# Patch attention and three 3x3 convolutions on one core: products without hold products, full products, and turning by scaled diagonals

## What is computed

```python
q = x @ Q_P;  k = stk @ K_P;  v = stk @ V_P      # stk: the 9 shifted views of x
alpha = softmax(sum(k * q) * mask, axis=-1)      # over the 9 neighbours
t = t_in = x + sum(alpha * v)
t = relu(conv(t, ff1) + b1)
t = relu(conv(t, ff2) + b2)
t = relu(conv(t, ff3) + b3)
return t_in + t
```

## Time and profile before

| | |
|---|---|
| median of 3 runs | 2381.85 us (2379.44 to 2382.46) |
| the profiled execution, its own time | 2380.99 us |
| its span | 2379.0 us |
| share of the span: TensorE, VectorE, ScalarE | 96%, 80%, 47% |
| loads of weights on TensorE (beside products) | 55% |
| granted clock of TensorE, mean | 0.993 of full |
| instructions | 65460 |
| 16 DMA engines, mean busy share | 46% |

### The profile page before, as it was taken

How to read it: one execution, slowest core, us unless ns; L and a number is a source line. 1 busy time by engine, 2 the same in 40 slices (tenths; PEclk the granted TensorE clock), 3 DMA queues, 4 the chain that set the end, 5 groups by cost and what they waited for, 6 DMA issues and landing times.

```text
span 2379.0 us, 65460 instructions
## 1 busy us (share of the span) xinstructions
PE 2287.5 (96%) x25180; PEld 1317.7 (55%) x25180; DVE 1895.5 (80%) x2851; ACT 1127.4 (47%) x3108; POOL 15.5 (1%) x24
## 2 busy tenths in 40 slices
PE   4999999999999999999999999999998999999998
PEld 2655555555565555555555555555555555555554
DVE  4888888887588888888768888888877888888886
ACT  1554455444454554454345544544535445444543
POOL 2000000000000000000000000000000000000000
PEclk9999999999899999999999999999999999999999
DMA  4444544544355445444344454445434544454443
GB/s 125 138 137 136 158 134 125 160 141 134 94 158 152 137 126 162 139 136 137 123 138 144 126 160 140 135 136 157 135 124 119 156 147 138 127 160 136 128 153 119
DMA packets 291286, 328.79 MB, mean 138 GB/s; under 512 B 89300, under 2 KB 223252, under 8 KB 284564
## 3 DMA queue, kind: packets, MB, share of 16 engines
q1 hardware_dynamic: 291164, 327.17, 46.4%
HBM read 152.50 MB, written 33.82 MB: 78 GB/s over the span
## 4 chain that ended last, share of the span: by engine, by line
PE 79%; DVE 12%; issue 5%; ACT 1%; DVEq 1%; DMA 1%; SPq 0%; ACTq 0%
PE conv_banks L476 28%; PE conv_banks L435 16%; PE conv_banks L490 15%; PE mix_bank L413 6%; PE score_banks L387 3%; DVE work L836 3%; PE score_banks L398 3%; PE mix_bank L425 3%; DVE dt L764 2%; DVE tf L746 2%; DVE dt L760 2%; PE score_banks L381 1%; PE proj_bank L420 1%; PE score_banks L395 1%; PE conv_banks L450 1%
## 5 line engine op out<-in xcount | busy, mean ns | idle before, releaser
L476 PE MATMUL conv_banks<-dodd,w3f 128*64 128x512 f32 (+1 forms) x1656 | 500.3, 579 | 6.2 <-DVE dodd L760 3.9
L476 PE MATMUL conv_banks<-deven,w3f 128*64 128x512 f32 (+1 forms) x1656 | 489.9, 566 | 0.0
L598 ACT ACTIVATE prob<-score_banks,negmax 128x100 f32<-128x100 f32 x1040 | 343.0, 343 | 273.4 <-DVE negmax L726 273.4
L435 PE MATMUL conv_banks<-dt,w1f 128*64 128x256 f32 (+3 forms) x4224 | 414.4, 384 | 0.0
L490 PE MATMUL conv_banks<-duh,w2h 64*128 64x512 f32 (+2 forms) x1632 | 362.2, 423 | 4.0 <-ACT m_sb L634 2.1
L664 ACT ACTIVATE relued<-work,bias 128x1024 f32<-128x1024 f32 (+2 forms) x136 | 150.4, 1108 | 435.7 <-DVE work L836 435.7
L490 PE MATMUL conv_banks<-duh,w2l 64*128 64x512 f32 (+2 forms) x1632 | 329.5, 382 | 0.0
L435 PEld LDWEIGHTS conv_banks<-dt,w1f 128*64 128x64 f32 (+1 forms) x4224 | 219.2, 135 | 138.6 <-issue 65.9
L490 PE MATMUL conv_banks<-dul,w2h 64*128 64x512 f32 (+2 forms) x1632 | 286.4, 383 | 0.0
L476 PEld LDWEIGHTS conv_banks<-dodd,w3f 128*64 128x64 f32 x1656 | 138.8, 137 | 226.5 <-issue 181.3
L490 PEld LDWEIGHTS conv_banks<-duh,w2h 64*128 64x128 f32 x1632 | 168.7, 185 | 137.7 <-issue 104.5
(11 more groups left out here) (97 smaller groups left out, 3224.2 us busy)
## 6 DMA issues: line engine op xcount, KB each, us to landing
xk<-x_keys SPq DMA_DIRECT2D x66, 800.0 KB
xc<-x_bands SPq DMA_DIRECT2D x66, 650.0 KB, 5.0
dodd<-dodd SPq DMA_DIRECT2D x68, 512.0 KB, 5.1
xr<-x_bands SPq DMA_DIRECT2D x264, 128.0 KB, 3.5
out<-work SPq DMA_DIRECT2D x60, 512.0 KB, 2.7
dt<-dt SPq DMA_DIRECT2D x68, 256.0 KB, 2.3
deven<-deven SPq DMA_DIRECT2D x68, 256.0 KB, 5.7
duh<-duh SPq DMA_DIRECT2D x68, 256.0 KB, 2.4
```

The source lines that it names most:

```text
L435: mm = nc.tensor.matmul(bank[(LOWER, UPPER)[o], n * 256 + lo * 64:n * 256 + hi * 64], w1f[i][rows, m, s, o * C:o * C + C], dt[rows, lo + s ...
L476: return nc.tensor.matmul(bank[rows, lo * 128:hi * 128], w3f[:, m, s, odd * C:odd * C + C], source[:, lo + s // 2:hi + s // 2, m], start=s ...
L598: last = nc.scalar.activation(prob[:, g % 2, a], score_banks[:, g % 2, a * KEYS:(a + 1) * KEYS], ACT.Exp, bias=negmax[:, g % 2, a:a + 1], ...
```

## The change

On TensorE the eight hold products of a step are dropped (single ones stay in the part ahead of the loop). The waits stand by themselves, and those of r, scores, turn and v-product are moved ahead of the last one or more products of what comes before. Of the third convolution tile 1 comes second and 2 third. In the second convolution, where both halves of the rows meet the same product, one full product of 128 by 128 takes the place of two halves: a tile has 6 full products (`begin2`: 4, `end2`: 2) and then 6 half products. `half_done` and its wait go.

`prob` is no longer scaled. VectorE forms one reciprocal for the 8 patches of a half and multiplies an identity with it, which gives 8 diagonal matrices `scaled` of 64 by 64; `turn` multiplies `prob` by them in an ordinary f32 product, where a transpose was. Two loads for the identity come into SP's queue ahead of the biases. On VectorE the outer part of `dt` is formed behind the first outer sum of the next step, and maxima, sums and scaling are put in another order; on ScalarE the copy of r comes first, the copy of the third convolution ahead of the first relu, and the copy of the second convolution's odd tile ahead of the copy of y.

```diff
-    return ORDER3.index(j) if which == CONV3 else 4 + 2 * j + (which == EVEN)
+    return j if which == CONV3 else 4 + 2 * j + (which == EVEN)
...
+            for rows in (LOWER, UPPER):
+                sp.dma_start(eye_two[rows], eye[rows, rows]).then_inc(const_in, 16)
...
+            def hold(bank):
+
+                nc.tensor.matmul(bank[:, 0:2], eye16_sb[:], window_sb[:, 0:2], start=True, stop=True)
+
+            def await_band(b):
+                pe.wait_ge(t_ready, b * 2)
+                pe.wait_ge(xc_in, b * 16 + 16)
+                pe.wait_ge(xs_in, b * 32 + 32)
...
+            def await_r(b, half):
+                pe.wait_ge(r_ready, b * 2 + (half + 1))
+                if half:
+                    pe.wait_ge(probt_ready, b * 2 + 1)
...
             def turn(b, half):
-                pe.wait_ge(prob_ready, b * GROUPS + (2 * half + 2))
-                nc.tensor.matmul(score_banks[:, 0, 0:2], eye_sb[LOWER], eye_sb[LOWER, 0:2], start=True, stop=True)
                 for a in range(HALF):
                     for n, rows in enumerate((LOWER, UPPER)):
-                        last = nc.tensor.transpose(score_banks[0:KEYS, n, a * C:(a + 1) * C],
-                                                   prob[rows, a // GROUP, a % GROUP], eye_sb[rows, rows])
+                        last = nc.tensor.matmul(score_banks[0:KEYS, n, a * C:(a + 1) * C],
+                                                prob[rows, a // GROUP, a % GROUP], scaled[rows, a],
+                                                start=True, stop=True)
...
-            def conv1(G, k, b, outer):
+            def conv1(G, k, b, outer, att=False):
...
-                nc.tensor.matmul(conv_banks[:, 2 * outer, 0:2], eye16_sb[:], window_sb[:, 0:2], start=True, stop=True)
                 streams = (0, 3) if outer else (2, 1)
                 for n, m in enumerate(streams):
                     for i in range(2):
+                        if att and n == 1 and i == 1:
+                            await_r(b, 0)
...
                 for w in (w2h, w2l):
-                    tap2(k, EVEN, j, LOWER, 0, w, duh, w is w2h, False)
-                    tap2(k, ODD, j, UPPER, 0, w, duh, w is w2h, False)
-
-            def go_on2(G, k, j):
-                for w in (w2h, w2l):
-                    tap2(k, EVEN, j, LOWER, 1, w, duh, False, False)
-                    tap2(k, ODD, j, UPPER, 1, w, duh, False, False)
+                    if ahead and w is w2l:
+                        ahead()
+                    tap2(k, EVEN, j, FULL, 0, w, duh, w is w2h, False)
+                    tap2(k, ODD, j, FULL, 1, w, duh, w is w2h, False)
+
+            def end2(G, k, j, ahead=None):
+
                 pe.wait_ge(du_low, G * 2 + (j // 2 + 1))
-                for s in range(2):
-                    even = tap2(k, EVEN, j, LOWER, s, w2h, dul, False, False)
-                    odd = tap2(k, ODD, j, UPPER, s, w2h, dul, False, False)
-                even.then_inc(half_done, 1)
-                odd.then_inc(half_done, 1)
-
-            def end2(G, k, j):
-                pe.wait_ge(half_done, G * 8 + (2 * j + 2))
+                tap2(k, EVEN, j, FULL, 0, w2h, dul, False, False)
+                tap2(k, ODD, j, FULL, 1, w2h, dul, False, False)
                 for n, (w, d) in enumerate(((w2h, duh), (w2l, duh), (w2h, dul))):
-                    odd = tap2(k, ODD, j, LOWER, 1, w, d, False, n == 2)
-                    even = tap2(k, EVEN, j, UPPER, 0, w, d, False, n == 2)
+                    if ahead and n == 2:
+                        ahead()
+                    odd = tap2(k, ODD, j, UPPER, 0, w, d, False, n == 2)
+                    even = tap2(k, EVEN, j, LOWER, 1, w, d, False, n == 2)
...
                 conv3_tile(G, k, 0)
-                conv3_tile(G, k, 2)
+                conv3_tile(G, k, 1, (lambda: await_inv(b, 0)) if att else None)
                 if att:
                     turn(b, 0)
-                conv3_tile(G, k, 1)
+                conv3_tile(G, k, 2, (lambda: await_r(b, 1)) if att else None)
...
                 begin2(G, k, 0)
-                go_on2(G, k, 0)
+                end2(G, k, 0)
                 if att:
                     mix(b, 0)
-                begin2(G, k, 1)
-                go_on2(G, k, 1)
+                begin2(G, k, 1, (lambda: await_inv(b, 1)) if att else None)
                 if att:
                     turn(b, 1)
-                end2(G, k, 0)
                 end2(G, k, 1)
                 if att:
                     mix(b, 1)
-                begin2(G, k, 2)
+                begin2(G, k, 2, (lambda: await_y(b)) if att else None)
                 if att:
                     v_product(b)
-                go_on2(G, k, 2)
                 begin2(G, k, 3)
-                go_on2(G, k, 3)
                 end2(G, k, 2)
-                end2(G, k, 3)
+                next_band = None if k == BANDS - 2 else b if k == BANDS - 1 else b + 1
+                end2(G, k, 3, None if next_band is None else lambda: await_band(next_band))
...
-            def scale(b, g):
-                dve.wait_ge(exp_done, b * GROUPS + (g + 1))
-                nc.vector.reciprocal(expinv[:, g % 2], expsum[:, g % 2]).then_inc(inv_done, 1)
-                dve.wait_ge(inv_done, b * GROUPS + (g + 1))
-                inv = expinv[:, g % 2].rearrange("q (a o) -> q a o", o=1).broadcast_to([128, GROUP, KEYS])
-                nc.vector.tensor_tensor(prob[:, g % 2], prob[:, g % 2], inv, ALU.mult).then_inc(prob_ready, 1)
+            def scale(b, half):
+                dve.wait_ge(exp_done, b * GROUPS + (2 * half + 2))
+                nc.vector.reciprocal(expinv[:], expsum[:].rearrange("q g a -> q (g a)")).then_inc(inv_done, 1)
+                dve.wait_ge(inv_done, b * 2 + (half + 1))
+                inv = expinv[:].rearrange("q (a o) -> q a o", o=1).broadcast_to([128, HALF, C])
+                ones = eye_two[:].rearrange("q (o n) -> q o n", o=1).broadcast_to([128, HALF, C])
+                nc.vector.tensor_tensor(scaled[:], ones, inv, ALU.mult).then_inc(inv_ready, 1)
...
                     outer(G, k - 1, ODD, 1)
+                if k < BANDS:
+                    t_inputs(None, b - 1, k % 2, 1)
+                if k:
                     outer(G, k - 1, EVEN, 1)
```

More of the change, by code:

```diff
@@ L357, in _ @@
         def _(pe):
+            def hold(bank):
[4 more added lines that the diff above has]
+                pe.wait_ge(xs_in, b * 32 + 32)
             def r_product(b):
-                if not isinstance(b, int):
-                    pe.wait_ge(t_ready, b * 2)
-                pe.wait_ge(xs_in, b * 32 + 32)
-                nc.tensor.matmul(proj_bank[:, 0:2], eye_sb[LOWER], eye_sb[LOWER, 0:2], start=True, stop=True)
                 near, far = xc[:, 1:1 + BAND, 1:65], xs[:]
@@ L415, in mix, with await_y @@
                 last.then_inc(mixed, 1)
+            def await_y(b):
+                pe.wait_ge(y_ready, b * 2 + 2)
             def v_product(b):
[L418 to L420 removed]
                 moving = y[:].rearrange("c a (r s) -> c a r s", s=PATCH)
@@ L461, in conv1, with conv3_tile @@
                             tap1(k, i, m, n, rows, o, 1 - o, n == 0 and k == BANDS, n == 1)
-            def conv3_tile(G, k, j):
+            def conv3_tile(G, k, j, ahead=None):
                 if G is ALL_STEPS:
@@ L484, in conv3_tile @@
                 tap(1, 1, False, False)
+                if ahead:
+                    ahead()
                 tap(0, 1, False, True)
@@ L492, in tap2, with begin2 @@
                                         d[rows, lo + s:hi + s, STREAMS[j]], start=start, stop=stop)
-            def begin2(G, k, j):
+            def begin2(G, k, j, ahead=None):
                 if j == 0:
@@ L532, in _ @@
             pe.wait_ge(xc_in, 16)
+            pe.wait_ge(xs_in, 32)
+            hold(proj_bank)
             r_product(0)
+            await_r(0, 0)
+            hold(score_banks[:, 0])
             scores(0, 0)
+            await_inv(0, 0)
+            hold(score_banks[:, 0])
             turn(0, 0)
+            await_r(0, 1)
+            hold(score_banks[:, 0])
             scores(0, 1)
             mix(0, 0)
+            await_inv(0, 1)
+            hold(score_banks[:, 0])
             turn(0, 1)
             mix(0, 1)
+            await_y(0)
+            hold(proj_bank)
             v_product(0)
@@ L542, in _ @@
             pe.wait_ge(pool_zeroed, 1)
+            await_band(1)
+            hold(conv_banks[:, 0])
             def step(G, k, b, att):
                 if att:
-                    pe.wait_ge(xc_in, b * 16 + 16)
                     r_product(b)
-                conv1(G, k, b, False)
+                conv1(G, k, b, False, att)
                 if att:
@@ L589, in _ @@
                 step(g0 + BANDS, BANDS, b0 + BANDS, True)
-            for j in ORDER3:
+            for j in range(4):
                 conv3_tile(ALL_STEPS, 0, j)
@@ L870, in _ @@
             dve.wait_ge(w_ready, 3)
-            for part in range(2):
```

(5 more changed lines are left out.)

57 lines of the change are left out of this document (26 added, 31 removed).

## The result

The changed kernel takes **2523.52 us** (median of 4 runs, 2521.59 to 2524.58), the kernel before 2381.57 in the same comparison: a ratio of 1.0596, 95% interval 1.0578 to 1.0615. That is slower by 142 us, where the forecast was slower by 105, 2487 us in 2405 to 2555. The profiled execution has a span of 2519.8 us. The 37 us between forecast and result are 0.57 us in each of the 64 steps with attention, and this is what the rest of the text is after.

A forecast was written before the change was run, and what follows sets the result against it. TensorE's queue was taken as the bound; terms of −1.09, −0.12, +0.78, +1.26, −0.20 and +0.99 sum to +1.62 us a step, times 64 is 104 us, giving 2487 us, range 2405 to 2555.

The forecast's parts named there:

- The stall in front of the inner first convolution, −0.46: TensorE's wait for VectorE's addition at L836: moving the dt subtraction behind it removes stall and hold, 0.46 us a step saved.
- Full products, −0.20: Second convolution: a full product takes 0.223 us, where a pair of halves takes 0.23; 0.20 us a step saved.
- The first turn's wait, −0.10: Waits in front of the first turn, outside the start: mostly go as VectorE gets its work sooner, 0.10 us a step saved.
- Turns, +0.78 and +1.26: Transposes become f32 products, 16 pairs at 0.088 us: first turn 0.78 us longer, second 1.26, with two changes of division.
- Changes of division, +0.99: Second convolution: five more switches a step between full and half rows of the array, 0.20 us each, add 0.99 us.
- Holds other than the inner one: Dropped hold products save 0.11 us each at r-product, outer first convolution and second scores, 0.20 at first scores.
- The v-product, −0.12: From mix to v-product 1.54 us without hold, with two products more: 0.12 us a step saved, about 0.2 idle remaining.
- The relief of VectorE at nothing: Cheaper scaling on VectorE saves some 0.6 us a half, but on an engine with spare time, so costed at nothing.
- (1): Turns: 100-column passes flow at 0.058 us a pair, loads don't pace them; −0.96 us a step, 2425 us; chance 0.13.
- (2): Turns: loading 100 columns takes as long as 128, 0.112 us a pair; +0.77 us a step, 2536 us; chance 0.13.
- (3): Borders between products: all 24 changes of division lose their 0.15 to 0.20 us; about 2220 us; chance 0.08.
- (4): Time stays as it is: free-flowing turns, full products at 0.215 us, no v-product stall; about 2390 us; chance 0.04.

The follow-up runs named there:

- e5_split_sum: Changed kernel with VectorE's outer sum of the odd tiles (128x1024) split into two of 128x512, the first needing tile 2 alone: 2509.86 us.
- e10_fewer_changes: Changed kernel with all full products of tiles 2 and 3 first, then all their half products, so two changes of division fewer: 2499.9 us.
- e8_widths: Changed kernel with 80 columns of weights loaded in a step's first turn and 128 in its second, instead of 100 in both: 2537.84 us.
- e7_r_twice: Changed kernel with the r-product issued twice in a row, the second over the first: 2572.97 us.
- e11_holds_back: Changed kernel with turn and second convolution undone, and eight 128 by 128 bf16 hold products put back: 2400.42 us.

## Why the prediction was right or wrong

**Direction and bound: right; the sum was short by a quarter.** TensorE's queue bounds both kernels, and two of the terms, the turns and the changes of division, made it slower. But 0.55 us a step was missing (2.17 against 1.62). Three terms promised savings that didn't come, and one cost less than forecast, which hid part of it; that part was luck.

**The stall in front of the inner first convolution, −0.46: failed.** It is 0.94 against 0.95, so nothing was saved, not even the hold's 0.11. The step that failed is "so L836 is ready some 1.14 earlier, at 1311.5". I took the instruction ahead of L836 for what held it, since VectorE was busy without a gap. But tile 3 held it nearly as long. In the changed kernel the sum starts 0.20 behind the first product that follows tile 3 (1387.43 to 1387.63); by that distance L836 could have started at 1311.31 and did at 1311.43. The row shows only the later of the two, and it was later by 0.12 us, not by 1.14. Asking what L836 reads, and when the last of it is written, would have shown this. With the sum split, 0.35 of it came (`e5_split_sum`).

**Full products, −0.20: failed.** The slot is 0.233, the upper of my ends (0.2335), and nothing was saved. I took the middle between 0.215 and 0.2335 when the nearest row, the pair of halves of the same type, said 0.23.

**The first turn's wait, −0.10 in the sum of the holds: failed.** I spread 10.3 us over 64 steps, but a steady step has no such wait, and 4.3 of the 10.3 us are one more wait ahead of the loop. In the loop it was 5.9 us in 8 places before, all at the edges of an image pair, and is 3.5 us in 4 places after: 2.4 us in the whole kernel, where 64 times 0.10 is 6.4.

**Turns, +0.78 and +1.26: the pace right, the second difference too large.** The pace was forecast as 0.088 by proportion to columns and is 0.088. The first turn takes 1.55 (forecast 1.58), so +0.75. The second takes 1.56 to the next start, 0.08 more ahead of it (1413.02 to 1413.57 is 0.55 for two slots of 0.23) and 0.10 behind it, as the next full product's weights are late: 1.74 (forecast 1.78). Undoing both gives back 1.95; the changes beside the second turn stay when only the transposes return. What was wrong is the old second turn, 0.52 in the forecast. The timeline of TensorE before, at its start and at the mix product behind it:

```profile
1336.65 0.16 PE L395 MATMUL score_banks<-eye_sb 64*128 64x2 f32 x1
...
1338.80 1.15 PE L413 MATMUL mix_bank<-probt,xk 100*64 100x64 f32 x32
```

Between them lie 2.15 us: six slots of 0.233, 0.10 for the change of division, and 0.65 for the turn. It left the two row groups 0.11 out of step (starts at 1337.12 and 1337.23), and the mix product comes behind the later one. So the difference is 1.74 − 0.65 = +1.09, 0.17 less than forecast.

**Changes of division, +0.99: right.** 0.20 each (`e10_fewer_changes`).

**Holds other than the inner one: right.** Without its hold the first scores' mask starts 2.79 behind the first convolution (1388.91 to 1391.70), with it 3.01 (1312.81 to 1315.82): 0.22, forecast 0.20. The r-product's first pair comes 0.33 behind the last half pair (1423.96 to 1424.29), where with the hold it came 0.44 behind (1310.88 to 1311.32); eight holds added back cost 1.02. **The v-product, −0.12: right.** It is 1.57 from mix to v against 1.54 forecast; 0.02 of the 0.03 is the slot of two full products, which is counted above. The idle time of 0.2 is where it was said to be. **The relief of VectorE at nothing: right**; its 0.5 us a step showed nowhere in the time.

With these, the sum is 1.62 + 0.45 (stall) + 0.20 (full products) + 0.10 (first turn's wait) − 0.03 − 0.17 (turns) = 2.17, and the step grew by 2.17; terms that are off by 0.04 or less, in both directions, are left out. The range's lower end, 82 us below the forecast, lies further out than the 74 that its two terms for that side give; nothing rested on it.

**The rivals.** (1), loads that don't pace the turn, wanted turns of 1.0 us: out. (2), a load of 100 columns as long as one of 128, would have given 2536, nearer to the 2523.5 measured than my 2487. By the total alone it would have passed for the cause; but it wanted turns of 1.9 us, and `e8_widths` shows 0.088 and 0.112 apart. (3), free changes of division, is refuted by the 0.34 inside each tile, where no wait stands. (4), as it is, fell with (1).

## What to carry to other kernels

When TensorE's queue is full, count what an edit adds in loaded columns and in changes of the array's division, not in products or multiplications: fewer and fuller products were slower here, because they alternate with half ones. A change costs 0.20 us here, nearly a whole slot of 0.233. An engine without gaps still isn't the cause of a wait by that alone; before a piece of its work is moved away, look at what the next instruction reads and when the last of it is ready. And take a change apart before judging it: this one held a gain of 1.9% under a loss of 6%, and with two small edits the gain became 3.9%.

## What the runs showed of the hardware that was not expected

- A pair of fp32r products of 64 rows and a full one of 128 rows take the same 0.233 us for 512 columns, the full one with or without gaps in its access pattern; full bf16 ones come to about 0.22.
- A pair of f32 passes on the two row groups with 64 moving columns costs its load alone, 0.83 ns a column and 5 ns; each product has two passes and pays twice.
- After some 5 us of idle time at a change of image pair the granted clock was 0.57 for 7.2 us (`e7_r_twice`). The step with that idle time in it took 35.60 to 38.16 at the second change in three kernels that differ elsewhere; how much of this is the clock no run shows.
- A hold product of 128 by 128 with two moving columns costs 0.11 us in a full queue, 0.22 between products that share a division, and nothing where TensorE stands anyway (`e11_holds_back`).
